# Two transformer blocks on one core: four stages' pipelines rewritten, the last stage's sum of residual and last bias on VectorE

## The chip, the cores and the metric

One of the eight cores of a Trainium2 chip runs the whole program. The metric is the device time of one execution in microseconds, lower is better. Three executions of the kernel before took 4201.59, 4202.47 and 4207.68 us; the median, 4202.47, is its time.

## The reference

Input x is 4 x 1024 x 512 in fp32 (4096 rows of 512). Block 0 is a transformer block: layer norm modulated by the condition, attention with 16 heads of 32 and a distance bias, output projection, layer norm, an MLP of 2048 with tanh gelu. Block 1 is of the same size with ternary weights and activations rounded to 8 bits by row:

```python
def act_quant(x):
    s = 127.0 / jnp.clip(jnp.max(jnp.abs(x), axis=-1, keepdims=True), EPS)
    return jnp.clip(jnp.round(x * s), -128, 127) / s
def bitlinear(x, w, b):
    return act_quant(x) @ weight_quant(w).T + b
...
# block 0, behind its attention
x = x + out @ Wout
h2 = layer_norm(x, ln2_g, ln2_b)
x = x + (gelu(h2 @ W1 + b1) @ W2 + b2)
# block 1
qkv = bitlinear(adaln(x, c, g1, w_ada1, b_ada1), w_qkv, b_qkv)
...
x = x + bitlinear(o, w_proj, b_proj)
h = gelu(bitlinear(adaln(x, c, g2, w_ada2, b_ada2), w_fc1, b_fc1))
x = x + bitlinear(h, w_fc2, b_fc2)
```

adaln is an RMS norm times g, times (1 + scale), plus shift; scale and shift are a bitlinear of the condition, one row per batch element.

## The kernel before, in words

The program is raw: each engine (TensorE "pe", VectorE "dve", ScalarE "act", GpSimd "pool", SyncE "sp" that issues all DMAs) has its own list of instructions in a fixed order, and waits on semaphores by hand. `settle` is an engine's wait for its own last counted result. Six stages follow one another with a barrier of all engines between them; results pass through scratch in HBM. Rows are handled in tiles of 128 x 512, 32 of them (NT), or in 8 blocks of 512 rows.

1. **A**, the first projection (about 0 to 320 us), and 2. **attention 0** (to 1410 us): not touched. 5. **Attention 1** (2714 to 3800 us): not touched.

3. `stage_mlp0` has two parts. **C**, `stage_outproj` (L684 to L860): for each tile, load the attention's rows o (L727) and x (L729), transpose o (L763), split it into a high and a low half (ScalarE L790, VectorE L812), twelve matmuls with the halves of Wout (L772), add x (VectorE L833), statistics (L835, L837), the root of the variance (start on VectorE L638, power on POOL L642, three more small steps on VectorE L647 to L651), normalise (L821), transpose (L779), gain and bias (four ScalarE passes, L800), high half on POOL (L854), low half on VectorE (L828), store both (L754). POOL also adds b2 to the residual (L849), and SP stores that as x1 (L745). Beside this, 18 pieces of weights (Wout, W1, W2, 512 KB each) are loaded into two raw buffers (L712) and split, high half on ScalarE (L717), low half on VectorE (L722), one piece every second step. In a step SP issues the tile's loads first, then the store of x1, then the piece's load, then the halves' stores. The split that uses the piece is in the same step. Low halves `lo` have three buffers.

**M**, `stage_fc0` (L863 to L1147): for each block of 512 rows, 16 slices f of the hidden width: twelve matmuls of fc1 (L989), gelu and high half on ScalarE (L1044, L1048), low half gl on VectorE (L1127), and two slices later twelve matmuls of fc2 into four accumulators (L1000). VectorE also works through a list of ternary weight pieces, one a slice (L1056 to L1081), whose loads SP issues one slice ahead (L926); for two of the weights TensorE has small matmuls of its own (L1020). At a block's end VectorE adds the four accumulators to x (L1133) and at once, through the one buffer xb2, x plus the projection's bias (L1140), each after the store of the one before. SP stores x2 and x2b alternately (`store_x2`, L974 to L981), ahead of the next piece's load.

4. **D**, `stage_qkv1` (L1253 to L1475): RMS norm, rounding, transposition and q, k, v for each tile. The bias enters as one more matmul in each sum: 6 rows, the products of three bf16 pieces of the bias (`bias_rows`, L1153) and three pieces of the inverse scale of the row (`inverse_pieces`, POOL, L1182). Its operands are `brow`, 6 x n, and `rT`, 6 x 128, which TensorE transposes from rc (L1295) and ScalarE copies (L1346), beside the copy of the rounded tile (L1347). The matmuls are L1303 (four) and L1304 (the bias).

6. **F**, `stage_mlp1` (L1478 to L1841): for each tile, round the attention's row (largest entry L1694, step L1699 and L1701, ScalarE L1627, VectorE L1713), transpose (L1550), project (L1559), add the residual (L1722), square (ScalarE), root on POOL (L1816 to L1824), times G, normalise (L1730, L1735), round, transpose (L1569, scales L1570), fc1 in two halves of two groups (L1581, each with a 3-row fp32 bias matmul L1582), gelu (L1657), round h (L1662, L1713), transpose in two halves (L1590), fc2 in two halves of eight matmuls (L1599), output (L1760). Three VectorE operations `scale` (L1704, L1751) multiply a step by the weight's mean; two (L1741, L1743) make the pieces of the inverse scale. POOL adds the last bias bf2 to the residual x3 into the output buffer (L1834). The bias of fc1 is split in two fp32r pieces by VectorE (L1807, L1809) in step 1, one row is placed by a DMA (L1529), and SP loads fc2's weights, three batch elements' G and shift, and tile 3 behind that. The lists run in steps s: at step s an engine handles tile s of its first job, and older tiles of later ones.

Of the kernel before, what the change touches and what calls it, by code (L numbers as in the profile page):

```python
# [636 lines left out]
def rstd_start(K, v, var, scale, eps, s_var):  # L637
    K.nc.vector.tensor_scalar(v, var, scale, eps, ALU.mult, ALU.add).then_inc(*s_var.up())  # L638


def rstd_pow(K, r, v, s_pow):
    K.nc.gpsimd.tensor_tensor(r, v, K.mhalf[:, 0:1], ALU.pow).then_inc(*s_pow.up())  # L642


def rstd_end(K, v, r, t):
    nc, dve = K.nc, K.dve
    nc.vector.tensor_scalar(t, r, r, v, ALU.mult, ALU.mult).then_inc(*dve.own.up())  # L647
    dve.settle()
    nc.vector.tensor_scalar(t, t, -0.5, 1.5, ALU.mult, ALU.add).then_inc(*dve.own.up())
    dve.settle()  # L650
    nc.vector.tensor_tensor(r, r, t, ALU.mult).then_inc(*dve.own.up())  # L651
    dve.settle()


# [30 lines left out]
def stage_outproj(K, w1h, w1l, w2h, w2l, raw_b):  # L685
    nc, a, pe, dve, act, pool, sp = K.nc, K.a, K.pe, K.dve, K.act, K.pool, K.sp
    with Stage(K, "C") as S:
# [3 lines left out]
        o_l, x_l = S.loads("oC", 3, [P, D]), S.loads("xC", 4, [P, D])  # L691
# [4 lines left out]
        st = [S.sb(f"statC{i}", [P, 12]) for i in range(4)]  # L696
        hT = [S.sb(f"hTC{i}", [P, DC, P]) for i in range(2)]
        hi, lo = S.stores("hChi", 3, [P, DC, P], F32R), S.stores("hClo", 3, [P, DC, P], F32R)
# [3 lines left out]
        s_To, s_oh, s_ol, s_mm, s_x, s_var, s_pow, s_xh, s_Tx, s_hT, s_hi, s_lo, s_xb = (S.sem() for _ in range(13))  # L702
# [21 lines left out]
        def load_tile(i):  # L724
            rows = slice(i * P, (i + 1) * P)
            o, s = o_l.take(sp, i, 1, (s_To, i + 1))
            nc.sync.dma_start(o[:], K.o_s[rows, :]).then_inc(*s.up(16))  # L727
            x, s = x_l.take(sp, i, 1, (s_xh, i + 1), (s_xb, i + 1))
            nc.sync.dma_start(x[:], a["x"].rearrange("b l d -> (b l) d")[rows, :]).then_inc(*s.up(16))  # L729

        def sync_program():
            load_w(0)
            load_tile(0)
            load_w(1)
            for dst, src in ((g2, a["L0_cond_ln2_g_cols"]), (b2, a["L0_cond_ln2_b_cols"]), (b2b, a["L0_cond_b2"].partition_broadcast(P))):
                nc.sync.dma_start(dst[:], src).then_inc(*s_vec.up(16))
            load_tile(1)
            for s in range(NT + 4):
                if s + 2 < NT:
                    load_tile(s + 2)  # L740
                if 0 <= s - 2 < NT:
                    i = s - 2
# [3 lines left out]
                if s % 2 == 0 and 2 + s // 2 < len(pieces_w):  # L746
                    load_w(2 + s // 2)
                if 0 <= s - 4 < NT:
                    i = s - 4
                    rows = slice(i * P, (i + 1) * P)  # L750
                    sp.wait_ge(s_lo, i + 1)
                    for buf_r, half in ((hi, "hi"), (lo, "lo")):
                        buf, sem = buf_r.of(i)
                        nc.sync.dma_start(K.h2_s[half][:, rows].rearrange("(c p) t -> p c t", p=P), buf[:].bitcast(F32)).then_inc(*sem.up(16))  # L754
            for r in (xb, hi, lo):
                r.done(sp)

        def tensor_program():
            for s in range(NT + 4):
                if s < NT:  # L760
                    ps, o = po_r.take(pe, s, (s_ol, s + 1)), o_l.ready(pe, s)
                    for c in range(DC):
                        op = nc.tensor.transpose(ps[:, c * P:(c + 1) * P], o[:, c * P:(c + 1) * P], K.ident[:])  # L763
                    op.then_inc(*s_To.up())
                if 0 <= s - 1 < NT:
                    i = s - 1
                    ps = pm_r.take(pe, i, (s_x, i + 1))
                    pe.wait_ge(s_ol, i + 1)
                    pe.wait_ge(s_wlo, 2)
# [1122 lines left out]
```

## Time and profile before

| | |
|---|---|
| median of three executions | 4202.47 us |
| the profiled execution | 4206.6 us, its span 4204.8 us |
| TensorE busy | 3877.2 us, 92% of the span |
| VectorE, ScalarE, POOL busy | 2793.8, 2670.9, 899.6 us |
| TensorE's mean granted clock | 0.957 of 2.4 GHz |
| DMA | 419.49 MB, mean 100 GB/s |

How to read it: PE is TensorE's matmuls, PEld its weight loads, which can run beside matmuls; DVE is VectorE, ACT ScalarE, SPq the DMA queue of SyncE. PEclk is the granted clock, 1.00 for 2.4 GHz and 0.50 for 1.2 GHz, or a mean of both over a stretch. A matmul's record is longer than the distance to the next one, because they are pipelined: the distance between starts is what one costs. "idle before" is the time an engine stood before the instruction, with the one it waited for.

### The profile page before, as it was taken

How to read it: one execution, taken by the hardware profiler on the slowest of the kernel's cores; microseconds unless marked ns; L12 is line 12 of the kernel's file. 1: busy time of each engine (PE TensorE's matmuls, PEld its weight loads, DVE VectorE, ACT ScalarE, POOL GpSimd, SP SyncE). 2: the span in 40 equal slices, each digit the busy share in tenths (PEclk: the TensorE clock that was granted, in tenths of full speed). 3: DMA queues.
4: the chain of work that ended last, by engine and by line, in shares of the span. 5: the costliest groups of instructions: out<-in, count | busy, mean ns of one | idle time of the engine just before them, and what ended most of it. 6: DMA issues, size and time to landing. Idle time of an engine off the chain costs nothing. (4 is left out here: it accounts for less than half of the span.)

```text
span 4204.8 us, 70173 instructions
## 1 busy us (share of the span) xinstructions
PE 3877.2 (92%) x26756; PEld 2571.4 (61%) x26756; DVE 2793.8 (66%) x5147; ACT 2670.9 (64%) x4699; POOL 899.6 (21%) x1188
## 2 busy tenths in 40 slices
PE   8998999999999755689999969799999999997999
PEld 7885666666666444577778854366666666663444
DVE  4327888888888565434431227688888888886887
ACT  2227888888888422222222217598888888885887
POOL 0005555555555222100000016400000000002221
PEclk9998999999999877899999989899999999997999
DMA  5445333323232355434431226732323323214221
GB/s 185 182 164 129 64 64 74 67 59 64 59 64 47 104 170 169 148 126 150 150 115 51 76 71 245 263 75 59 64 61 73 69 59 64 59 29 136 69 70 43
DMA packets 307495, 419.49 MB, mean 100 GB/s; under 512 B 89365, under 2 KB 165673, under 8 KB 307159
## 3 DMA queue, kind: packets, MB, share of 16 engines
q1 hardware_dynamic: 307162, 415.00, 35.4%
q8 instruction: 215, 3.52, 0.4%
q14 instruction: 118, 0.97, 0.1%
HBM read 257.31 MB, written 157.32 MB: 99 GB/s over the span
## 5 line engine op out<-in xcount | busy, mean ns | idle before, releaser
L555 ACT ACTIVATE Sn<-Sn,mn 128x1024 f32<-128x1024 f32 x1024 | 1174.8, 1147 | 30.4 <-DVE mn L583 18.7
L521 PEld LDWEIGHTS pt<-ident,Sn 128*128 128x128 f32 x8192 | 880.9, 141 | 420.9 <-issue 412.9
L521 PE MATMUL pt<-ident,Sn 128*128 128x128 f32 x8192 | 1123.6, 280 | 1.6 <-DVE PT L547 0.9
L545 ACT ACTIVATE PT<-pt 128x512 f32<-128x512 f32 x1280 | 737.2, 597 | 236.9 <-PE pt L521 236.8
L489 PE MATMUL sp<-KS,QS 97*128 97x512 f32 (+1 forms) x2048 | 733.8, 440 | 44.4 <-DMA KS<-s_khi 22.9
L583 DVE CUSTOM_DVE_ANT_0 Sn<-sp,biastile 128x1024 f32<-128x1024 f32 x512 | 624.5, 1220 | 145.1 <-PE sp L489 113.5
L585 DVE TENSOR_SCALAR_CACHE_REDUCE Sn<-sp 128x1024 f32<-128x1024 f32 x512 | 624.3, 1220 | 136.6 <-PE sp L489 136.4
L628 POOL TENSOR_SCALAR biastile<-dist,ascale 128x1024 f32<-128x1024 f32 x512 | 573.9, 1121 | 499.7 <-DVE mn L583 484.9
L510 PE MATMUL po<-PT,Vp 128*32 128x256 f32 x8192 | 651.5, 391 | 0.0
L547 DVE COPY PT<-pt 128x512 f32<-128x512 f32 x768 | 531.3, 692 | 118.5 <-PE pt L521 118.5
L1044 ACT ACTIVATE gf<-pf,b1T 128x512 f32<-128x512 f32 x128 | 88.1, 688 | 562.0 <-PE pf L989 535.9
L1208 POOL TENSOR_TENSOR Gada<-Gada,gada 128x512 f32<-128x512 f32 x8 | 10.1, 1268 | 1915.5 <-DMA Sada<-s_emb 1915.5
L510 PEld LDWEIGHTS po<-PT,Vp 128*32 128x32 f32 x8192 | 163.1, 108 | 343.6 <-issue 341.2
L1127 DVE TENSOR_TENSOR gl<-gf,gh 128x512 fp32r<-128x512 f32 x128 | 88.4, 693 | 381.8 <-ACT gh L1048 380.0
L489 PEld LDWEIGHTS sp<-KS,QS 97*128 97x128 f32 (+1 forms) x2048 | 312.0, 193 | 48.2 <-issue 42.3
L1000 PE MATMUL pacc<-w2h,gh 128*128 128x512 f32 x512 | 204.9, 400 | 13.4 <-DVE gl L1127 13.4
L1000 PE MATMUL pacc<-w2l,gh 128*128 128x512 f32 x512 | 204.9, 400 | 0.0
L1000 PE MATMUL pacc<-w2h,gl 128*128 128x512 f32 x512 | 204.5, 399 | 0.0
L555 ACT ACTIVATION_READ_ACCUMULATOR Sn<-Sn,mn 128x1 f32 x1024 | 201.3, 197 | 0.0
L772 PE MATMUL pCm<-wo_hi,oChi 128*128 128x512 f32 x128 | 51.6, 540 | 122.9 <-DVE oClo L812 122.9
L362 DVE SCALAR_TENSOR_TENSOR qstage<-pA,qstage 128x512 fp32r<-128x512 f32 x64 | 44.2, 690 | 165.0 <-ACT qstage L298 165.0
L989 PE MATMUL pf<-mhi,w1h 128*128 128x512 f32 x512 | 143.6, 403 | 0.0
(230 smaller groups left out, 4923.3 us busy)
## 6 DMA issues: line engine op xcount, KB each, us to landing
QS<-s_qhi SPq DMA_DIRECT2D x128, 256.0 KB, 5.1
KS<-s_khi SPq DMA_DIRECT2D x128, 256.0 KB, 7.1
KS<-s_klo SPq DMA_DIRECT2D x64, 256.0 KB, 6.1
QS<-s_qlo SPq DMA_DIRECT2D x64, 256.0 KB, 6.9
Vp<-s_v SPq DMA_DIRECT2D x64, 256.0 KB, 7.9
s_o<-og SPq DMA_DIRECT2D x32, 512.0 KB, 8.7
xA<-in_x SPq DMA_DIRECT2D x8, 1024.0 KB, 5.8
s_qhi<-qstage SPq DMA_DIRECT2D x32, 256.0 KB, 2.0
```

Of the source, the lines that this page charges most:

```text
L489: op = nc.tensor.matmul(ps[:, g * BLK:(g + 1) * BLK], qs[0:rows_s, j, t * P:(t + 1) * P], ks[0:rows_s, j, g * BLK:(g + 1) * BLK], start=Tr ...
L510: op = nc.tensor.matmul(po[g * HD:(g + 1) * HD, :], v[:, kb, j * HD:(j + 1) * HD], pT[n % 2][:, kb, g * QW:(g + 1) * QW], start=kb == 0, s ...
L521: op = nc.tensor.transpose(ps[:, i, :], sn[:, (g * HALF + i) * P:(g * HALF + i + 1) * P], K.ident[:])
L545: nc.scalar.activation(dst, src, ACT.Copy).then_inc(*s_cp_act.up())
L547: nc.vector.tensor_copy(dst, src).then_inc(*s_cp_dve.up())
L555: nc.scalar.activation(sn[:], sn[:], ACT.Exp, scale=-1.0, bias=mn[n % 3][:, t:t + 1], accum_out=sums[n % 5][:, t:t + 1]).then_inc(*s_exp.up())
L583: nc.vector.tensor_tensor_reduce(sn[:], sp_r.at[s][:], bt[s % 2][:], 1.0, 3.4e38, ALU.add, ALU.min, m).then_inc(*s_min.up())
L585: nc.vector.tensor_scalar(sn[:], sp_r.at[s][:], 1.0, None, ALU.mult, ALU.min, m).then_inc(*s_min.up())
L628: nc.gpsimd.tensor_scalar(bt[s % 2][:], dist[:, t, :], K.ascale[:, n % H:n % H + 1], 1.0, ALU.mult, ALU.mult).then_inc(*s_bias.up())
L989: op = nc.tensor.matmul(ps[:], w[:, d, f * P:(f + 1) * P], x[:, d, :], start=n + d == 0, stop=n == 2 and d == DC - 1)
L1000: op = nc.tensor.matmul(pacc[t][:], x[:, t * P:(t + 1) * P], w[:, f, :], start=f == 0 and n == 0, stop=f == FC - 1 and n == 2)
L1127: nc.vector.tensor_tensor(gl[u % 3][:], gf[u % 2][:], gh[u % 3][:], ALU.subtract).then_inc(*s_gl.up())
```

## The change

The work computed is the same. Part by part:

- **C**: SP issues a weight piece's load one split ahead and first in the step (piece 3 + s/2 at even s; the split of 2 + s/2 is unchanged). Loads of o and x are issued apart, three and two steps ahead, at the step's end; x has five buffers. The whole inverse root goes to POOL (five operations, `inverse_root`), whose other job is the sum x + b2. The high half of the normalised tile goes from POOL to ScalarE. Consumers are moved to later steps (TAIL 9 for 4). `lo` has two buffers instead of three, the statistics eight instead of four.
- **M**: the four sums x + bias are made one a step in steps 2 to 5 of the next block (`with_bias`), their stores (`store_x2b`) likewise. After the last block SP first issues the four stores of x2, then the four of x2b. The load of x moves from step 4 to step 8 of a block.
- **D**: the bias matmul has 128 rows, all but six of them zero. `brow` is 128 x 1536 and is cleared by a VectorE memset ahead of the split, rc is 128 x 128, cleared once by POOL, and is transposed and copied with the tile as a fifth block of xT; `rT` and its copy go.
- **F**: the same for fc1's bias, now in D's form: three bf16 pieces, 128 rows, `brow` 128 x 2048. The two pieces of the inverse scale (VectorE) become D's five POOL operations; the three `scale` operations go from VectorE to POOL. The sum of x3 and bf2 goes from POOL to VectorE, behind `times_g`. VectorE's list is reordered and each job works on an older tile; ScalarE's order of round_o, copy_oT and copy_hT changes; TensorE's steps are renumbered; TAIL 8 for 7.

```diff
@@ C: sync_program
-            load_tile(1)
-            for s in range(NT + 4):
-                if s + 2 < NT:
-                    load_tile(s + 2)
...
+            load_o(2)
+            load_w(2)
+            for s in range(NT + TAIL):
+                if s % 2 == 0 and 3 + s // 2 < len(pieces_w):
+                    load_w(3 + s // 2)
...
-                if s % 2 == 0 and 2 + s // 2 < len(pieces_w):
-                    load_w(2 + s // 2)
...
+                if s + 3 < NT:
+                    load_o(s + 3)
+                if s + 2 < NT:
+                    load_x(s + 2)
@@ C: vector_program, after
+            for s in range(NT + TAIL):
+                if 0 <= s - 2 < NT:
+                    i = s - 2
+                    dve.wait_ge(s_x, i + 1)
+                    nc.vector.bn_stats(st[i % 8][:, 0:6], x_l.at[i][0][:]).then_inc(*s_bn.up())
+                if s < NT:
+                    o_low(s)
...
+                if s % 2 == 0 and 2 + s // 2 < len(pieces_w):
+                    split_lo(2 + s // 2)
+                if 0 <= s - 6 < NT:
+                    h_low(s - 6)
+                if 0 <= s - 1 < NT:
+                    residual(s - 1)
+                if 0 <= s - 3 < NT:
+                    normalise(s - 3)
@@ M: store_x2, store_x2b, with_bias
+                nc.sync.dma_start(K.x2_s[rows_of(i, t), :], x_l.at[i, t][0][:]).then_inc(*s_xst.up(16))
+
+        def store_x2b(i, t):
+            sp.wait_ge(s_xb, TPB * i + t + 1)
+            nc.sync.dma_start(K.x2b_s[rows_of(i, t), :], xb2[:]).then_inc(*s_xbst.up(16))
...
+                if u >= FC + 2 and 0 <= u % FC - 2 < TPB:
+                    with_bias(u // FC - 1, u % FC - 2)
@@ bias_rows
-    rows, rest = S.sb("brow" + name, [6, n], BF16), S.sb("brest" + name, [6, n])
+    rows, rest = S.sb("brow" + name, [P, n], BF16), S.sb("brest" + name, [6, n])
...
+        nc.vector.memset(rows[:], 0.0).then_inc(*dve.own.up())
@@ D: project
-            nc.tensor.matmul(pr[w][:], rT[i % 2][:], brow[:, cols], start=False, stop=True).then_inc(*s_m[w].up())
+            nc.tensor.matmul(pr[w][:], xT[i % 2][:, DC, :], brow[:, cols], start=False, stop=True).then_inc(*s_m[w].up())
@@ F: times_g and gpsimd_program
             nc.vector.tensor_tensor(xn[i % 3][:], x3[i % 4][:], G[:, b, :], ALU.mult).then_inc(*s_xg.up())
+            dve.wait_ge(s_bf2, 16)
+            buf = xo.room(dve, i)
+            nc.vector.tensor_tensor(buf[:], x3[i % 4][:], bf2[:], ALU.add).then_inc(*s_xb.up())
...
-                nc.gpsimd.tensor_tensor(buf[:], x3[i % 4][:], bf2[:], ALU.add).then_inc(*s_xb.up())
```

In F, VectorE's list after the change is, in step s: largest_o(s), quantise h(s-6), quantise x(s-4), largest_h(s-5, 0), times_g(s-3) with the new sum, largest_h(s-5, 1), step_o(s), step_h(s-5), normalise(s-3), output(s-7), largest x(s-3), quantise o(s-1), step x(s-3), residual(s-2), and in step 1 the bias split at the end. TensorE's is: turn_h(s-4, 0), turn_x(s-2), fc2(s-5, 1), turn_o(s), fc1(s-2, 0), turn_h(s-4, 1), project(s), fc1(s-2, 1), fc2(s-4, 0).

## Rows read from the trace of the kernel before

**Rows 1.** Windows of stages C, M, D, F: length, busy (instructions), PEclk, DMA share, GB/s.

```profile
1405.00:1715.00 310.00, 161.76 (x690) 127.95 (x679) 175.94 (x340) 81.50 (x179) 76.29 (x96) 0.74 0.56 169
1715.00:2490.00 775.00, 731.64 (x3108) 588.11 (x3108) 241.79 (x356) 170.19 (x257) 0.00 (x0) 0.97 0.31 105
2490.00:2710.00 220.00, 172.19 (x896) 76.66 (x896) 149.99 (x296) 136.00 (x288) 126.39 (x356) 0.89 0.68 249
...
3795.00:4204.80 409.80, 378.72 (x2138) 175.26 (x2130) 324.99 (x742) 296.95 (x386) 93.39 (x196) 0.95 0.27 82
```

**Rows 2.** Waits in stage C, 1440 to 1680 us: total, times, longest.

```profile
ACT w1h L717 <- DMA wraw<-in_L_cond_W: 94.3, 7, 14.1
```

**Rows 3.** Timeline of stage C: start, us, what, idle before.

```profile
1541.22 0.42 SPq L712 DMA_DIRECT2D wraw<-in_L_cond_W  x1
...
1545.79 1.06 ACT L717 ACTIVATE w2h<-wraw 128x1024 fp32r<-128x1024 f32 x1 [13.20 <-DMA wraw<-in_L_cond_W]
```

**Rows 4.** Groups by line, stage C, 1440 to 1680 us: busy, mean ns, idle before.

```profile
L833 DVE TENSOR_TENSOR xC<-pCm,xC 128x512 f32<-128x512 f32 x27 | 18.4, 682 | 0.0
...
L722 DVE TENSOR_TENSOR w2l<-wraw,w2h 128x1024 fp32r<-128x1024 f32 x7 | 8.6, 1226 | 47.0 <-ACT w2h L717 47.0
```

**Rows 5.** The transpositions of o in stage C: ns min/median/max, first and last start.

```profile
L763 PE MATMUL pCo<-ident,oC x128: 272/273/475, 1416.8 to 1685.1; 128*128 128x128 f32 x128
```

**Rows 6.** Waits of TensorE in stage M, 1715 to 2490 us.

```profile
PE pacc L1000 <- DVE gl L1127: 13.4, 3, 5.2
PE pmisc L1020 <- DVE tern L1081: 11.8, 1, 11.8
```

**Rows 7.** Timeline at the end of stage M.

```profile
2488.34 0.32 SPq L981 DMA_DIRECT2D s_x2b<-xb  x1
...
2490.47 0.69 DVE L1140 TENSOR_TENSOR xb<-xM,bpb 128x512 f32<-128x512 f32 x1 [2.15 <-DMA s_x2b<-xb]
```

**Rows 8.** Timeline of one tile's step in stage D.

```profile
2620.21 0.40 PE L1294 MATMUL pxD<-identb,xqD 128*128 128x128 bf16 x4
...
2622.57 0.09 PEld L1304 LDWEIGHTS pqD<-browD,rTD 6*128 6x128 bf16 x1 [0.42 <-issue]
...
2622.89 1.04 PE L1303 MATMUL pkD<-wtqkv,xTD 128*128 128x512 bf16 x4
...
2625.47 0.40 PE L1294 MATMUL pxD<-identb,xqD 128*128 128x128 bf16 x4
```

**Rows 9.** The chain that ended last, one tile of stage F: start, share in us.

```profile
4054.29 1.83 PE p2F L1599 x8
...
4056.90 1.73 PE p2F L1599 x8
...
4064.23 0.97 PE pwF L1581 x4
4065.20 0.42 PE pwF L1582
4065.62 1.83 PE p2F L1599 x8
```

**Rows 10.** Groups by line of VectorE, stage F, 4000 to 4100 us.

```profile
L1730 DVE TENSOR_TENSOR xnF<-x3F,Gada 128x512 f32<-128x512 f32 x9 | 6.1, 682 | 0.0
...
L1704 DVE TENSOR_SCALAR smF<-smF,wmean 128x1 f32<-128x1 f32 x27 | 5.4, 200 | 0.0
```

**Rows 11.** Windows in stage F's head and steady part, columns as rows 1.

```profile
3820.00:3880.00 60.00, 49.72 (x223) 20.56 (x223) 45.20 (x110) 38.38 (x54) 15.77 (x34) 0.77 0.40 129
...
4020.00:4090.00 70.00, 70.00 (x400) 32.96 (x400) 61.73 (x144) 56.98 (x76) 18.06 (x40) 1.00 0.27 76
```

**Rows 12.** Timeline of stage F's head.

```profile
3817.15 2.28 DVE L1809 TENSOR_TENSOR blowF<-brawF,browF 3x2048 fp32r<-3x2048 f32 x1
...
3833.90 0.69 DVE L1694 TENSOR_REDUCE smF<-oF 128x1 f32<-128x512 f32 x1 [7.45 <-DMA oF<-s_o]
...
3839.72 0.40 PE L1569 MATMUL pxF<-identb,xqF 128*128 128x128 bf16 x4 [0.58 <-DVE xqF L1713]
```

More of the change, by code:

```diff
@@ new lines, in turn_o, with project @@
+        def turn_o(i):
+            ps, o = po_r.take(pe, i, (s_ol, i + 1)), o_l.ready(pe, i)
+            for c in range(DC):
+                op = nc.tensor.transpose(ps[:, c * P:(c + 1) * P], o[:, c * P:(c + 1) * P], K.ident[:])
+            op.then_inc(*s_To.up())
+        def project(i):
+            ps = pm_r.take(pe, i, (s_x, i + 1))
+            pe.wait_ge(s_ol, i + 1)
+            pe.wait_ge(s_wlo, 2)
+            for n, (x, w) in enumerate(((oh[i % 2], wo_hi), (oh[i % 2], wo_lo), (ol[i % 2], wo_hi))):
+                for d in range(DC):
+                    op = nc.tensor.matmul(ps[:], x[:, d, :], w[:, d, :], start=n + d == 0, stop=n == 2 and d == DC - 1)
+            op.then_inc(*s_mm.up())
@@ new lines, in turn_h @@
+        def turn_h(i):
+            ps = px_r.take(pe, i, (s_hT, i + 1))
+            pe.wait_ge(s_xh, i + 1)
+            for c in range(DC):
+                op = nc.tensor.transpose(ps[:, c * P:(c + 1) * P], xh[i % 2][:, c * P:(c + 1) * P], K.ident[:])
+            op.then_inc(*s_Tx.up())
+        def tensor_program():
+            for s in range(NT + TAIL):
+                if 0 <= s - 2 < NT:
+                    project(s - 2)
+                if 0 <= s - 5 < NT:
+                    turn_h(s - 5)
+                if s < NT:
+                    turn_o(s)
@@ new lines, in o_high, with affine @@
+        def o_high(i):
+            act.wait_ge(s_To, i + 1)
+            if i >= 2:
+                act.wait_ge(s_mm, i - 1)
+            nc.scalar.activation(oh[i % 2][:], po_r.at[i][:].rearrange("p (c t) -> p c t", t=P), ACT.Copy).then_inc(*s_oh.up())
+        def affine(i):
+            act.wait_ge(s_vec, 48)
+            if i >= 2:
+                act.wait_ge(s_lo, i - 1)
+            act.wait_ge(s_Tx, i + 1)
+            for c in range(DC):
+                op = nc.scalar.activation(hT[i % 2][:, c, :], px_r.at[i][:, c * P:(c + 1) * P], ACT.Identity,
+                                          bias=b2[:, c:c + 1], scale=g2[:, c:c + 1])
+            op.then_inc(*s_hT.up())
@@ L782, in scalar_program, with h_high @@
+        def h_high(i):
+            buf = hi.room(act, i)
+            act.wait_ge(s_hT, i + 1)
+            nc.scalar.activation(buf[:], hT[i % 2][:], ACT.Copy).then_inc(*s_hi.up())
         def scalar_program():
@@ L856, in stage_outproj @@
+        def gpsimd_program():
+            pool.wait_ge(s_vec, 48)
+            for i in range(NT):
+                inverse_root(i)
+                buf = xb.room(pool, i)
+                nc.gpsimd.tensor_tensor(buf[:], x_l.at[i][0][:], b2b[:], ALU.add).then_inc(*s_xb.up())
         sync_program()
@@ L955, in sync_program @@
                     store_x2(i - 1)
+                if i > 0 and 0 <= f - 2 < TPB:
+                    store_x2b(i - 1, f - 2)
                 if u + 1 < len(work):
@@ L1452, in gpsimd_program @@
         def gpsimd_program():
+            for buf in rc:
+                nc.gpsimd.memset(buf[:], 0.0).then_inc(*pool.own.up())
+            pool.settle()
             pool.wait_ge(s_winv, 1)
@@ L1621, in tensor_program @@
                     fc2(s - 5, 1)
+                if s < NT:
+                    turn_o(s)
+                if 0 <= s - 2 < NT:
+                    fc1(s - 2, 0)
+                if 0 <= s - 4 < NT:
+                    turn_h(s - 4, 1)
+                if s < NT:
+                    project(s)
+                if 0 <= s - 2 < NT:
+                    fc1(s - 2, 1)
+                if 0 <= s - 4 < NT:
+                    fc2(s - 4, 0)
         def round_o(i):
```

382 lines of the change are left out of this document (164 added, 218 removed).

## The prediction

> **What bounds the kernel now.** Read the windows first, one for each stage that the change edits, because a share over the whole span would mix six stages [rows 1]. Together the four take 1714.8 of 4204.8 us; the rest, the first projection and the two attentions, isn't touched and is taken at no change. The profiled execution took 4206.6 us (span and 1.8 us around it); that is 4.1 above the median of 4202.5, so I work against 4206.6 and take 4.1 off at the end.
>
> The four rows differ in kind. Stage C (output projection) keeps nobody busy: TensorE 162 of 310 us at a granted clock of 0.74, VectorE 176, DMA share 0.56. M, D and F keep TensorE busy for 94%, 78% and 92%. So C must be read for a wait, D and F for TensorE's cost per tile.
>
> C's waits: ScalarE stands 94.3 us before seven splits of W1's pieces, waiting for the piece's load, and W2's pieces alternate with them [rows 2]. The timeline shows why: the load is issued at 1541.22 and ScalarE starts 4.6 us later, having stood 13.2 us [rows 3]. SP issues it behind the tile loads and a store that wait on results of the last step, and the split that needs it stands ahead of the step's other work. First to last transposition takes 1685.1 - 1416.8 = 268.3 us, 8.65 a tile [rows 5].
>
> **Part 1, stage C.** The load is now issued one split (two steps) ahead, at the head of a step; VectorE's chain for the inverse root goes to POOL, with later consumers. The 13 us wait goes. What is late next? Per tile:
> - DMA: 0.56 x 310 = 174 us, 5.4 a tile at a share of 1. Same bytes afterwards.
> - TensorE: 161.8 x 0.74 = 120 us at full clock, 3.7 a tile; about 7.5 if granted only 1.2 GHz.
> - VectorE: five passes near 0.7 (two low halves, the residual, the statistics, the normalisation), half a split of 1.23, aggregation 0.2: 4.3 [rows 4].
> - ScalarE 81.5/32 = 2.5, plus a high half that it takes from POOL, 0.6: 3.1. POOL 76.3/32 = 2.4, less that pass, plus four small operations: near 3.
>
> DMA is highest. I take 6.0 us a tile (DMA share 0.9); ends 5.4 and 7.0. Gain 31 x 2.65 = 82. After the last transposition the stage now runs on for 30 us with split waits in it; I estimate 22. **C: -90** (-108 to -55). The ring of low halves is cut from three to two; its store has about two steps to land, so I cost it at nothing, and at steps under 5.4 it would bind first.
>
> **Part 2, stage M.** At each block's end VectorE makes four biased sums through one buffer, each behind the last one's store. TensorE loses 11.8 + 13.4 us behind that at four block ends [rows 6]. The sums move to the next block's steps, one a step. SP, however, still stores the four residual tiles one after another ahead of the next weight load, so only the sums' share goes: the third sum and store repeat after 2.13 + 0.69 + 0.03 = 2.85 us [rows 7], stores alone after about 2.1 + 0.35. With the last pair's store gone too, some 4 us a block end return: -15 for four. At the stage's end it turns round. Now all four residual stores (3 x 2.45 more) come before the first of the biased ones, still 2.85 apart: the last is issued about 5 us later than now, with no work to hide it. **M: -10** (-17 to +2). The later load of the residual tile (step 8) has seven steps for a load of a few us: nothing.
>
> **Part 3, stage D.** The bias matmul has 6 rows, afterwards 128 (zeros below). Its weight load comes after 0.42 us of idle, instead of during the matmul before, and from it to the next group pass 2622.89 - 2622.57 = 0.32 us [rows 8], where a matmul of this width takes 1.73/8 = 0.216 [rows 9]. The group before it ends 0.1 late too, as 0.97 for 0.86 in rows 9. So 0.2 is lost, three times a tile. D's step, 2625.47 - 2620.21 = 5.26, falls by 0.6 to 4.66. Cover: VectorE 150/32 = 4.7 busy (its head split included), POOL 3.9, ScalarE 4.2 less one small copy, DMA 0.68 x 220/32 = 4.7 [rows 1]. All are near, so I take 4.75: 31 x 0.5 = 15.5. The new memset of 128x1536 before the bias split lies on the head's path: no row shows it; nearest are passes of 0.7 to 1.2, lower bound 0, upper 2, taken 1.5. The 128-column transposition of the scales costs nothing visible. **D: -14** (-20 to -3).
>
> **Part 4, stage F.** TensorE's order of work is the same sequence, only its steps are renumbered. Its cost per tile is the distance of two equal rows of the chain, 11.33 us [rows 9], with TensorE busy 70 of 70 us at clock 1.00 [rows 11]. The 3-row fp32 bias matmul takes 0.42 for 0.216, and what follows it pays 0.10: four matmuls 0.97 for 0.86, eight 1.83 for 1.73 [rows 9]. That is 0.30 four times a tile: -1.20, and 0.05 for the fp32 transposition of the scales. TensorE then needs 10.08: 32 x 1.25 = **-40**.
>
> Does VectorE follow? It is busy 61.7 of 70 us, 9.99 a tile [rows 11]. It loses two pieces of the inverse scale and three scales, about 0.2 each (-1.0), and gains the sum of residual and last bias, 0.68 as the product of the same shape [rows 10]: 9.7. So it still lies under 10.08, by 0.4. On POOL, 93 of 410 us busy [rows 1], that sum has room; on VectorE it costs 0.68 of the scarcest cover, but nothing on the path while TensorE bounds. I add 0.1 a tile for this nearness: **+3**.
>
> The head loses. The bias for fc1 is now split in three pieces: memset, two casts, two subtractions over 2048 columns instead of one each. A subtraction takes 2.28 [rows 12], a cast about half: 7.0 against 3.5. A memset comes on top, which no row shows: 0.3 to 2.28 as that subtraction, taken 1.3. It starts some 1.5 earlier, ahead of the second residual. So it ends 3 later. SP waits for it, then places three rows (not one), and only then loads fc2's weights, the modulation rows and tile 3. VectorE already stands 7.45 us for tile 3, until 3833.90 [rows 12]; I get 3838.5. In the kernel before, tile 1's transposition is then ready at 3839.7. In the longer pipeline tile 0 is only normalised behind tile 3's reduction, some ten passes, 7 us. Its fc1 and a projection follow, 24 matmuls at 1.2 GHz, 0.43 each: 10 us. Only then comes tile 1, at 3855.8, 16 us later with nothing to hide it: **+16** (5 to 22). **F: -21** (-36 to +2).
>
> **Sum.** -90 - 10 - 14 - 21 = -135: 4206.6 - 135 = 4071.6, less 4.1: 4067 us.
>
> **A rule against parts 3 and 4.** The rows show the short weight load standing idle. The Trainium skill, "TensorE: Matmul & The Clock Gate", "LDWEIGHTS (loading the stationary operand)", says that a load costs by its columns, not its rows; by that alone 128 rows for 6 gain nothing. The same page, in the steps of a matmul, lets a load run ahead when row groups don't conflict or it goes to the background buffer, which leaves the gap unexplained. By the rule alone the sum would be rival 1's.
>
> **Rivals.**
> 1. *The padded matmul keeps its gap.* For it: both shapes have 128 columns. Against: loads of full height run ahead in the same stream, and a group's four matmuls keep 0.216. Then D and F lose 15 + 40 of their gains: 4067 + 55 = 4122. Chance 0.03.
> 2. *VectorE bounds F.* POOL's thirteen operations are those that D has, 3.9 us a tile. If 1.6 of that delays VectorE, a tile takes 11.3 and F gains nothing but its head: +37, 4104. Against: D's VectorE keeps up under the same load. 0.12.
> 3. *C at the low clock.* If the gaps keep TensorE often at 1.2 GHz, or SP's waits hold back transfers, a tile takes 7.0: +31, 4098. For it: clock 0.74 now. 0.14.
> 4. *Better.* C at 5.4 and a head that hides: -18 - 16, 4033. 0.10.
> 5. *Slower.* Stage F falls to the low clock and stays: at a mean grant c a tile takes 10.08/c. F's head had 0.77 while TensorE was busy 50 of 60 us [rows 11]. At 0.5 it is 20.2 a tile, +284 + 16 against 114 gained elsewhere: about 4390. It decides from 10.08/c = 14.4, c = 0.70. Against: TensorE stays over 95% busy in the steady part. 0.01.
>
> Forecast: 0.60. A measurement of this kernel can tell about 0.2% (8 us) from no change. The four terms' ends add up to 4021 and 4148, were all to fall one way, which isn't likely; the range 4028 to 4108 leaves out rival 1, rival 5 and a little of each tail. Faster 0.98, same 0.01, slower 0.01.
>
> **What would show it.** C: transpositions 6.0 apart, no ScalarE wait for weight loads of over 1 us, DMA share near 0.9. M: the 11.8 wait down to 8, last biased store 5 later after the last matmul. D: 4.7 a tile, no idle before L1304's successor. F: 10.1 to 10.2 a tile, TensorE full, VectorE waiting under 0.5 a tile, second tile's transposition about 53 us after the stage's first load (now 37). I am wrong if C's step stays over 7, or if F's is over 10.6.

## The result, and the profile of the kernel after

The kernel after takes 4012.8 us (median of four runs, 4008.7 to 4015.2) against 4202.7 for the kernel before (4201.6 to 4207.7): a ratio of 0.9545, with a 95% interval of 0.9528 to 0.9561. It is 190 us faster. The forecast was 135 us faster, 4067 with a range of 4028 to 4108; the result lies 15 us below the range. The profiled execution took 4015.2 us, its span is 4013.4.

Counted from one stage's first transfer to the next one's, in the two profiled executions (us):

| stage | before | after | difference | forecast |
|---|---|---|---|---|
| C | 303.3 | 171.5 | -131.8 | -90 |
| M | 783.5 | 764.3 | -19.2 | -10 |
| D | 214.9 | 200.8 | -14.1 | -14 |
| F | 401.9 | 373.8 | -28.1 | -21 |
| all others | 2501.2 | 2503.0 | +1.8 | 0 |

Nine tenths of the miss lie in C and M, and three quarters of it in C alone. How far a stage moves from kernel to kernel without any edit to it is told by the kernels below that are the kernel after except in another stage: C 168 to 174, M 762 to 769, F 372 to 376.

The windows of the four stages in the kernel after, to be read beside [rows 1], with the same columns:

```profile
1407.00:1587.00 180.00, 135.29 (x682) 101.60 (x674) 128.91 (x212) 102.14 (x211) 116.62 (x192) 0.91 0.91 291
1587.00:2342.00 755.00, 725.01 (x3108) 583.07 (x3108) 241.51 (x357) 170.60 (x257) 0.00 (x0) 0.98 0.32 108
2342.00:2552.00 210.00, 151.40 (x896) 83.65 (x896) 148.46 (x296) 136.37 (x257) 128.29 (x358) 0.87 0.75 264
3632.00:4013.40 381.40, 331.06 (x2130) 172.66 (x2122) 317.84 (x616) 293.78 (x354) 172.21 (x422) 0.93 0.27 88
```

C changed its kind: the DMA share went from 0.56 to 0.91, the clock from 0.74 to 0.91. And here is the first sign of what was wrong: share times length is 164 us, where the forecast had taken 174 as a quantity that no edit could lower, and the rate rose from 169 to 291 GB/s, more than the share did.

C's transpositions (durations, first and last start; [rows 5] before) and its longest waits, 1440 to 1555 us:

```profile
L751 PE MATMUL pCo<-ident,oC x128: 270/273/476, 1418.5 to 1559.1; 128*128 128x128 f32 x128
```

```profile
ACT oChi L783 <- PE pCo L751: 20.4, 25, 2.1
...
DVE hClo L823 <- DMA s_h2lo<-hClo: 20.0, 13, 2.6
ACT hTC L791 <- DVE hClo L823: 18.4, 19, 1.7
POOL xbC L879 <- DMA s_x<-xbC: 13.0, 14, 1.7
```

A tile takes 140.6 / 31 = 4.53 us, not 6.0. The wait of ScalarE for weight pieces is gone [rows 2]. What ends waits now is a store: VectorE stands for a buffer of low halves until its store has landed (20.0 us), and ScalarE stands behind VectorE for nearly as long. POOL stands 13.0 us for a buffer of its sum x + b2, until that store has landed, and for nothing else but its own last results.

The end of M [rows 7]:

```profile
2332.95 0.40 PE L1033 MATMUL pacc<-w2h,gl 128*128 128x512 f32 x1
2334.06 0.68 DVE L1144 TENSOR_TENSOR xb<-xM,bpb 128x512 f32<-128x512 f32 x1
2338.68 9.19 SPq L1014 DMA_DIRECT2D s_x2b<-xb  x4
2341.12 0.69 DVE L1144 TENSOR_TENSOR xb<-xM,bpb 128x512 f32<-128x512 f32 x1 [6.38 <-DMA s_x2b<-xb]
...
2349.95 0.32 SPq L1285 DMA_DIRECT2D xD<-s_x  x1
```

The second biased sum waits 6.38 us, because the first one's store is issued behind four residual stores. From the last matmul to the next stage's first transfer pass 17.0 us (12.8 before).

F's chain, the starts of the same group of eight matmuls in two tiles ([rows 9] before), and its head ([rows 12]):

```profile
3867.49 0.86 PE pwF L1612 x4
3868.36 0.22 PE pwF L1613
3868.57 1.73 PE p2F L1630 x8
...
3878.60 1.73 PE p2F L1630 x8
```

```profile
3639.57 0.34 SPq L1544 DMA_DIRECT2D oF<-s_o  x1
...
3652.03 0.91 DVE L1201 MEMSET browF<- 128x1024 uint32 x1 [0.16 <-issue]
...
3675.58 0.69 DVE L1725 TENSOR_REDUCE smF<-oF 128x1 f32<-128x512 f32 x1 [13.55 <-DMA oF<-s_o]
...
3681.76 0.61 PE L1600 MATMUL pxF<-identb,xqF 128*128 128x128 bf16 x4 [15.85 <-DVE xqF L1741]
...
3691.57 0.39 PE L1600 MATMUL pxF<-identb,xqF 128*128 128x128 bf16 x4
```

A tile takes 10.03 us for 11.33, every group of four matmuls 0.86 and every bias matmul 0.22. The second tile's transposition comes 52.0 us after the stage's first transfer (36.8 before).

### The profile page after: what moved, and what is told of

Same layout as the page of the kernel before. It is cut to its first block and busy times, and to the rows that moved or that the text cites. A ratio compares the mean times of both kernels' runs of the same rounds, so it can differ in the third digit from the quotient of the medians.

```text
span 4013.4 us, 70190 instructions
## 1 busy us (share of the span) xinstructions
PE 3777.5 (94%) x26756; PEld 2544.7 (63%) x26756; DVE 2737.7 (68%) x4895; ACT 2689.1 (67%) x4667; POOL 1023.3 (25%) x1512
## 5 line engine op out<-in xcount | busy, mean ns | idle before, releaser
L1077 ACT ACTIVATE gf<-pf,b1T 128x512 f32<-128x512 f32 x128 | 88.3, 690 | 536.2 <-PE pf L1022 526.9
```

## The experiments

Each kernel was compared with the kernel before on the same chip. The stages are parted by barriers, so a kernel is read by its own stage's length: the total alone would blur it by the 2 to 6 us that the other stages move. In the code, `...` marks what is left out.

**1. Is C's gain the wait for the weight pieces?** One kernel is the old one with the load moved alone, the other the new one with the load put back.

```diff
@@ wait_alone, from the kernel before
+            load_w(2)
             for s in range(NT + 4):
+                if s % 2 == 0 and 3 + s // 2 < len(pieces_w):
+                    load_w(3 + s // 2)
...
-                if s % 2 == 0 and 2 + s // 2 < len(pieces_w):
-                    load_w(2 + s // 2)
@@ wait_back, from the kernel after
-            load_w(2)
             for s in range(NT + TAIL):
-                if s % 2 == 0 and 3 + s // 2 < len(pieces_w):
-                    load_w(3 + s // 2)
...
+                if s % 2 == 0 and 2 + s // 2 < len(pieces_w):
+                    load_w(2 + s // 2)
```

> The kernel before with one edit: a weight piece's load is issued one split earlier and first in its step; order of work, root of the variance and rings as before. Theory 1 (the wait for pieces is nearly all of C's loss, so DMA transfers then carry the step): C falls from 303 us to 190 or less, the whole by 100 to 130 us. Theory 2 (the wait hides a second loop of nearly its length, the chain statistics, root, normalise, transpose, split across four engines, which the longer pipeline cuts): C only falls to 230 to 260, the whole by 40 to 70 us.

> The kernel after with one edit undone: the piece's load is issued in the step of its split again, behind the store of x1. Theory 1: the split waits some 8 us every second step again, C goes from 171 us to 270 or more, the whole 100 to 130 us slower than the kernel after (ratio to before 0.98 or more). Theory 2: the longer pipeline has most of the gain, C stays at 200 to 230 (ratio 0.962 to 0.970).

wait_alone: 4105.7 us, ratio 0.9764 (0.9749 to 0.9778), C 201.6 us. wait_back: 4075.5 us, 0.9694 (0.9679 to 0.9708), C 233.9. Neither theory in its pure form: from 303 us the load alone gives 102 and the rest of the edit alone 69, and both together 132. wait_alone by itself is already 12 us below what the forecast had for the whole of C (201.6 for 213). Its transpositions come 169.1 / 31 = 5.45 us apart. Here is its window 1450 to 1540, and under it four of VectorE's groups there (busy, mean ns, idle before):

```profile
1450.00:1540.00 90.00, 67.16 (x318) 52.58 (x317) 85.52 (x169) 40.25 (x88) 37.84 (x49) 0.94 0.89 279
```

```profile
L651 DVE TENSOR_TENSOR statC<-statC 128x1 f32<-128x1 f32 x16 | 11.8, 735 | 0.6
...
L647 DVE TENSOR_SCALAR statC<-statC 128x1 f32<-128x1 f32 x16 | 4.4, 273 | 1.1
...
L649 DVE TENSOR_SCALAR statC<-statC 128x1 f32<-128x1 f32 x16 | 2.5, 154 | 0.6
L638 DVE TENSOR_SCALAR statC<-statC 128x1 f32<-128x1 f32 x16 | 2.5, 154 | 0.6
```

VectorE is busy 85.5 of 90 us. The four small operations of the inverse root, which the change gives to POOL, take 21.2 / 16 = 1.3 us a tile, more than half of it in a product of one column (735 ns; the last section shows that this is mostly a wait for POOL). With the wait for pieces gone, VectorE is the next bound. Taking 1.3 us a tile from it is what these rows name as the way below 5.45; no kernel moves the chain alone, so how the other 30 us (201.6 to 171.5) part between the chain, the later consumers and the deeper buffers isn't shown.

**2. What sets 4.53 us?** Three theories: the rate of all transfers, the two buffers of low halves, VectorE. One kernel stores less, one more, one has three buffers again, and one has both.

```diff
@@ less_bytes (VectorE's wait for the buffer goes too; M loads the high halves twice)
-                    for buf_r, half in ((hi, "hi"), (lo, "lo")):
+                    for buf_r, half in ((hi, "hi"),):
...
@@ more_bytes (a buffer of xb is free when both stores have landed)
-        xb = S.stores("xbC", 2, [P, D])
+        xb = S.stores("xbC", 2, [P, D], n_dma=2)
...
                     nc.sync.dma_start(K.x1_s[i * P:(i + 1) * P, :], buf[:]).then_inc(*sem.up(16))
+                    nc.sync.dma_start(K.x2_s[i * P:(i + 1) * P, :], buf[:]).then_inc(*sem.up(16))
@@ lo3; lo3_more is lo3 with the edit of more_bytes
-        st = [S.sb(f"statC{i}", [P, 12]) for i in range(8)]
+        st = [S.sb(f"statC{i}", [P, 12]) for i in range(4)]
-        hi, lo = S.stores("hChi", 3, [P, DC, P], F32R), S.stores("hClo", 2, [P, DC, P], F32R)
+        hi, lo = S.stores("hChi", 3, [P, DC, P], F32R), S.stores("hClo", 3, [P, DC, P], F32R)
...
```

> The kernel after without the store of h2's low halves in C (M reads the high halves twice, so it moves the same bytes; the low term of h2 is left out of the output). C moves 44.0 MB for 52.4. Theory DMA (bytes at full rate set the step): transpositions 3.8 us apart for 4.53, C 22 to 25 us shorter. Theory ring (the two low buffers' wait sets the step): also shorter, as the wait goes with the store. Theory VectorE (its passes set the step): under 5 us.

> The kernel after with the sum x + b2 stored twice in C (the second time to the place of x2, which is written again later): 60.8 MB for 52.4. Theory DMA: 5.25 us a tile, C 22 to 25 us longer. Theory ring: some 0 to 10 us longer, by later landings alone. Theory VectorE: under 3 us.

> The kernel after with three buffers for the low halves in C again (the statistics get four instead of eight, which nothing waits for). Theory ring (the landing of a store into one of two buffers sets the step of 4.53 us): the step falls to VectorE's 4.1, C 10 to 13 us shorter. Theory rate (all transfers together are at their limit, the ring only shows it): step 4.4 to 4.5, C 0 to 4 us shorter.

> Three buffers for the low halves as in lo3, and x + b2 stored twice as in more_bytes: 60.8 MB in C. Theory rate (the transfers of the core are at a limit near 380 GB/s, which lo3 at 4.23 us a tile and 1.64 MB has just reached): 1.90 MB a tile take 5.0 us, C 22 to 25 us longer than in lo3. Theory ring (only buffers that wait for landings, here the two of x + b2, set the step, and VectorE else): 4.3 to 4.6 us a tile, C 2 to 12 longer than in lo3.

The fifth column is the mean from the first to the last transposition. The sixth is the mean of 20 tiles in the middle, between the ends of POOL's 9th and 29th sum x + b2, where nearly every tile has all its transfers; the last is what POOL stands in it, a tile, for a store of that sum to land.

| kernel | total, us | ratio (95%) | C, us | us a tile | middle tiles | POOL's wait for the store |
|---|---|---|---|---|---|---|
| after | 4012.8 | 0.9545 (0.9528 to 0.9561) | 171.5 | 4.53 | 4.69 | 0.50 |
| less_bytes | 4001.2 | 0.9519 (0.9505 to 0.9534) | 156.7 | 4.11 | 4.21 | 0.01 |
| more_bytes | 4029.0 | 0.9579 (0.9563 to 0.9595) | 187.3 | 5.01 | 5.27 | 1.12 |
| lo3 | 4002.7 | 0.9526 (0.9511 to 0.9540) | 163.2 | 4.23 | 4.34 | 0.14 |
| lo3_more | 4022.9 | 0.9571 (0.9557 to 0.9586) | 178.7 | 4.73 | 5.00 | 0.91 |

The step follows the bytes, but by 15 us where the rate theory asked for 22 to 25; and the third buffer alone gives 8 (10 in the whole, where the two intervals overlap; in C, 163.2 lies clear of the 168 to 174 of kernels without an edit there). Both the ring and the transfers have a part. The windows 1450 to 1540 of after, lo3 and less_bytes:

```profile
1450.00:1540.00 90.00, 77.63 (x387) 58.13 (x385) 72.43 (x124) 59.53 (x124) 71.51 (x117) 1.00 1.00 326
```

```profile
1450.00:1540.00 90.00, 82.52 (x418) 63.61 (x418) 84.05 (x136) 64.72 (x136) 76.54 (x124) 1.00 1.07 359
```

```profile
1450.00:1540.00 90.00, 84.46 (x432) 66.36 (x430) 88.30 (x138) 67.53 (x143) 79.59 (x128) 1.00 0.98 310
```

In less_bytes transfers no longer fill the time (310 GB/s). VectorE is busy 88.3 of 90 us there. But none of the three theories names POOL, which since the change has a list of six operations a tile in C. The group of its sum in the same window, in after, less_bytes and the kernel of the next experiment (busy, mean ns, idle before):

```profile
L879 POOL TENSOR_TENSOR xbC<-xC,b2b 128x512 f32<-128x512 f32 x19 | 25.5, 1342 | 9.9 <-DMA s_x<-xbC 9.8
```

```profile
L879 POOL TENSOR_TENSOR xbC<-xC,b2b 128x512 f32<-128x512 f32 x22 | 28.8, 1308 | 1.0 <-DMA s_x<-xbC 0.8
```

```profile
L883 POOL TENSOR_TENSOR xbC<-xC,b2b 128x512 f32<-128x512 f32 x21 | 27.1, 1292 | 0.0
```

POOL's other idle time is 0.08 to 0.11 us before each small operation, its `settle`. It never stands for an input in the middle tiles: with the settles its list fills everything but the wait for a store, 4.20 us a tile in after (4.69 - 0.50), in less_bytes and in lo3. So less_bytes, at 4.21, runs at the pace of that list, and its 15 us are what lies between after and that pace. How much of the 4.20 is POOL's own isn't known, because VectorE and POOL also hold each other up (last section). In lo3 the transfers have 359 GB/s for 326, and VectorE is busy 84 us; its other 6.0 are a wait for POOL's inverse root:

```profile
L835 DVE TENSOR_SCALAR xhC<-xC,statC 128x512 f32<-128x512 f32 x21 | 22.7, 1081 | 6.0 <-POOL statC L872 6.0
```

Does VectorE hold lo3? The next kernel takes work from it.

**3. Is it VectorE in lo3?** The normalisation goes to ScalarE.

```diff
@@ norm_act, from lo3 (POOL makes w = -mean * r)
-            nc.vector.tensor_scalar(xh[i % 2][:], x_l.at[i][0][:], t[:, 6:7], t[:, 9:10], ALU.subtract, ALU.mult).then_inc(*s_xh.up())
+            nc.scalar.activation(xh[i % 2][:], x_l.at[i][0][:], ACT.Identity, bias=t[:, 10:11], scale=t[:, 9:10]).then_inc(*s_xh.up())
...
```

> lo3 with the normalisation of C moved from VectorE to ScalarE (one activation with scale and bias, POOL makes the bias in one more small operation). VectorE loses 1.08 us a tile of 3.95 busy. Theory VectorE bounds lo3: step falls from 4.23 to 3.9 or less, C 10 us or more shorter. Theory rate: step stays at 4.1 to 4.25, C within 4 us of lo3. ScalarE then has 3.3 to 3.7 us a tile.

4007.6 us, 0.9538 (0.9523 to 0.9554), C 164.4, the tile (1546.6 - 1415.2) / 31 = 4.24 us. VectorE fell to 76.2 of the 90 us, and nothing came of it. Its window:

```profile
1450.00:1540.00 90.00, 81.71 (x420) 64.92 (x419) 76.23 (x115) 76.11 (x158) 78.53 (x146) 1.00 1.06 360
```

The rate is 360 GB/s again. So less work on VectorE alone doesn't shorten the step. It doesn't clear VectorE wholly, because the edit also gives POOL a seventh operation, and POOL is now full: its sum has 0.0 idle before it, and its list takes 4.33 us a tile in the middle, the whole step (lo3: 4.34, of which the list 4.20 and the store 0.14). What is shown is that two things stand at the step of lo3 at once, POOL's list and, by the next experiment, the rate.

**4. The disputed term by itself.** Three stages of nothing but C's transfers run ahead of C, each transfer waiting for the last one of its own buffer only.

```diff
@@ moves, from the kernel after
+        stage_moves(K, w1h, raw_b, "Z", dict(o=3, x=5, b=2, h=3, l=2))
+        stage_moves(K, w1h, raw_b, "Y", dict(o=3, x=5, b=2, h=3, l=3))
+        stage_moves(K, w1h, raw_b, "X", dict(o=6, x=6, b=6, h=6, l=6))
         stage_outproj(K, w1h, w1l, w2h, w2l, raw_b)
```

> The kernel after with three extra stages ahead of C that only move C's bytes (per tile: o and x loaded, x1 and both halves stored, half a weight piece: 1.57 MB, in C's shapes, zeros stored), each transfer waiting only for the last one of its own buffer: first with C's rings (two low-half buffers), then with three of them, then with six of everything but the weights. They measure the disputed term itself. The prediction's floor: 5.4 us a tile in all three. Theory ring: the first takes 4.3 to 4.5 us a tile, the second 3.9 to 4.2, the third 3.5 to 4.0, and C's 4.53 and lo3's 4.23 stand just above the first and second. Theory rate: all three within 0.2 of each other, at 4.1 to 4.3, and C's 4.53 comes from the way the transfers are spread in time. If all three are under 3.9, transfers by themselves set neither, and the loop of waits through the engines does.

The issues of x1's stores in the three stages, and the windows between the first and the last of them (one execution, 4471.7 us in all, the three stages in it):

```profile
L705 SPq DMA_DIRECT2D s_x<-bZ x32: 429/549/1538, 1416.2 to 1552.3; - x32
...
L705 SPq DMA_DIRECT2D s_x<-bY x32: 432/524/1443, 1566.4 to 1704.0; - x32
...
L705 SPq DMA_DIRECT2D s_x<-bX x32: 441/606/1359, 1723.5 to 1859.7; - x32
```

```profile
1416.20:1552.30 136.10, 0.00 (x0) 0.00 (x0) 0.00 (x0) 0.00 (x0) 0.00 (x0) 0.50 1.06 353
1566.40:1704.00 137.60, 0.00 (x0) 0.00 (x0) 0.00 (x0) 0.00 (x0) 0.00 (x0) 0.50 1.06 351
1723.50:1859.70 136.20, 0.00 (x0) 0.00 (x0) 0.00 (x0) 0.00 (x0) 0.00 (x0) 0.50 1.07 352
```

136.1 / 31 = 4.39 us a tile, 4.44 and 4.39: the same with two, three or six buffers, at 351 to 353 GB/s. That is a rate, not a ring, and it stands at a share of 1.06, not at 1. Beside work the core moved a little more: 359 in lo3, 360 in norm_act, 366 in lo3_more, in the same window. Now the middle tiles can be read. In lo3 a tile takes 4.34 us, about what the bare transfers take, and just above POOL's 4.20. After, with two low buffers, takes 4.69 at 326 GB/s. A second store makes 1.84 MB a tile, for which the bare rate asks 5.1 us (worked out: 4.39 x 1.84 / 1.57); more_bytes takes 5.27 and lo3_more 5.00. The means between first and last transposition lie lower, because that stretch has fewer bytes a tile: the stores lag four to seven tiles behind, and the last weight piece is issued in step 28. Why work beside the transfers goes with a slightly higher rate stays open.

The Trainium skill, "DMA: Bandwidth & Descriptors", "Where 436 GB/s comes from", gives about 358 GB/s as one core's share of HBM and says that this binds transfers between HBM and SBUF, with a larger value for a core alone; the 351 to 366 GB/s of the runs here lie near the 358, though only one core is at work.

**5. M: are the block ends the biased sums?** They go back to the block's end, stored by turns.

```diff
@@ m_back, from the kernel after
-                    store_x2(i - 1)
-                if i > 0 and 0 <= f - 2 < TPB:
-                    store_x2b(i - 1, f - 2)
+                    store_pairs(i - 1)
...
+                    for t in range(TPB):
+                        with_bias(i, t)
-                if u >= FC + 2 and 0 <= u % FC - 2 < TPB:
-                    with_bias(u // FC - 1, u % FC - 2)
```

> The kernel after with M's four biased sums at the block's end again and stored by turns with the residual tiles (the later load of the residual stays). Theory of the prediction, sized by the stage: the other seven block ends cost 23 us again, the last one 4 less: M 19 us longer than after, the whole 4032. Rival: the later load of the residual tile has part of the 23: M only 8 to 15 longer.

4029.8 us, 0.9588 (0.9574 to 0.9602), 17 more than after, and M 782.4 us, 18 more. The later load of the residual has no part that can be seen. TensorE's waits in M, first of after, then of m_back ([rows 6] has 13.4 and 11.8):

```profile
PE pmisc L1053 <- DVE tern L1114: 7.8, 1, 7.8
PE pacc L1033 <- DVE gl L1168: 1.0, 2, 0.6
```

```profile
PE pacc L1037 <- DVE gl L1172: 14.3, 3, 5.2
PE pmisc L1057 <- DVE tern L1118: 11.5, 1, 11.5
```

The three waits of 13.4 us in all shrink to 1.0 in after and come back whole.

**6. D and F: is it the height of the bias matmul?** Both operands are cut to the six rows that aren't zero, and nothing else.

```diff
@@ short_rows, from the kernel after; the same in D
-                op = nc.tensor.matmul(pw[n][:, g * D:(g + 1) * D], xT[i % 2][:, DC, :], brow[:, cols], start=False, stop=True)
+                op = nc.tensor.matmul(pw[n][:, g * D:(g + 1) * D], xT[i % 2][0:6, DC, :], brow[0:6, cols], start=False, stop=True)
```

> The kernel after with the bias matmuls of D and F reading only the six rows that are not zero (both operands cut to six rows, the zeros stay where they are). Theory gap (a short weight load isn't drawn ahead, 0.2 us lost for each): D's tile 0.5 longer, 15 us in all, as before the change; F's four a tile make 10.03 into 10.8, 25 us; the whole 35 to 42 us slower than after. Theory that the row count does nothing: under 2 us, and the gain of D and F came from their other edits.

4052.2 us, 0.9639 (0.9623 to 0.9655), 39 more than after. The two stages have 36 of it: F 398.2 for 373.8, D 211.9 for 200.8. A stretch of F's timeline in short_rows, then in after:

```profile
3861.74 0.09 PEld L1613 LDWEIGHTS pwF<-browF,xTF 6*128 6x128 bf16 x1 [0.42 <-issue]
3861.74 0.39 PE L1613 MATMUL pwF<-browF,xTF 6*128 6x512 bf16 x1
3862.06 1.04 PE L1612 MATMUL pwF<-wtfc,xTF 128*128 128x512 bf16 x4
```

```profile
3863.43 0.10 PEld L1613 LDWEIGHTS pwF<-browF,xTF 128*128 128x128 bf16 x1
3863.65 0.38 PE L1613 MATMUL pwF<-browF,xTF 128*128 128x512 bf16 x1
3863.86 1.03 PE L1612 MATMUL pwF<-wtfc,xTF 128*128 128x512 bf16 x4
```

The short load starts with its own matmul, behind 0.42 us of standing; the full one 0.22 ahead of it, beside the matmul before. By the starts, 0.32 us pass to the next group for 0.21, and the group ahead is 0.1 longer too (0.97 for 0.86 in F's chain). Both loads last the same, 0.09 and 0.10 us: the rule of the Trainium skill, "TensorE: Matmul & The Clock Gate", "LDWEIGHTS (loading the stationary operand)", that a load costs by its columns, agrees with these records. It doesn't tell when the load starts, and that is the only difference that these rows show.

**7. The sum on VectorE or on POOL.** The part of the change that its name mentions is undone alone.

```diff
@@ pool_sum, from the kernel after: out of times_g, into gpsimd_program behind inverse_root
-            nc.vector.tensor_tensor(buf[:], x3[i % 4][:], bf2[:], ALU.add).then_inc(*s_xb.up())
+                    nc.gpsimd.tensor_tensor(buf[:], x3[(s - 3) % 4][:], bf2[:], ALU.add).then_inc(*s_xb.up())
```

> The kernel after with the sum of residual and last bias in F on POOL again, behind the inverse root. Theory TensorE bounds F: VectorE falls from 67 to about 62 of 70 us busy and the stage's steady tile stays 10.03; the whole within 3 us. Theory nearness (VectorE at 96% holds TensorE up in places): 3 to 6 us faster. Theory POOL late (its small operations for the steps come later behind the sum, and it slows VectorE at the port): 5 to 30 us slower.

4015.0 us, 0.9554 (0.9539 to 0.9568), F 372.8 us: no difference. 70 us of F's steady part in after and in pool_sum:

```profile
3850.00:3920.00 70.00, 70.00 (x456) 37.11 (x454) 67.06 (x133) 62.93 (x76) 36.95 (x91) 1.00 0.25 77
```

```profile
3853.00:3923.00 70.00, 70.00 (x456) 37.11 (x454) 62.58 (x127) 62.95 (x78) 38.59 (x100) 1.00 0.27 80
```

VectorE goes from 67.1 to 62.6 us and TensorE stays at 70 of 70. VectorE at 96% costs nothing here (the totals, 4015.0 and 4012.8, are within each other's intervals).

**8. Three repairs together.**

```diff
@@ v_all, from the kernel after: lo3's edit in C, and
@@ M: the last block's stores, x2 and x2b of each tile by turns
-            store_x2(NBLK - 1)
-            for t in range(TPB):
-                store_x2b(NBLK - 1, t)
+            store_pairs(NBLK - 1)
@@ F: sync_program
+            load_tile(3)
             place_bias()
+            load_tile(4)
...
-            for s in range(NT + TAIL):
+            for s in range(2, NT + TAIL):
```

> The kernel after with three repairs, one for each stage: lo3 in C; after M's last block the stores of residual and biased sum by turns as before the change; in F tile 3 is loaded ahead of the placing of the bias rows and tile 4 ahead of fc2's weights. By stages: C 8 to 10 shorter, M 4 to 5 shorter (from the last matmul to the next stage 12.8 us for 17.0). F: theory that tile 3's landing holds the head: VectorE's 13.6 us of waiting for it go and F falls from 374 to 360 to 365; theory that the bias split, the weights and the longer pipeline hold it: F within 3 us. The whole 3987 to 4000.

3989.0 us (3986.1 to 3991.1), ratio 0.9491 (0.9477 to 0.9506): the fastest, 24 us under after, their intervals apart. C 162.4, M 760.5, F 362.5. From M's last matmul to the next stage it is 12.8 us again (2333.44 - 2320.66). F's head, where the stage's first transfer is at 3624.63:

```profile
3653.56 0.61 PE L1608 MATMUL pxF<-identb,xqF 128*128 128x128 bf16 x4 [3.70 <-DVE xqF L1749]
```

The first tile's transposition comes 28.9 us after it (42.2 in after), and F gets 11.3 of those 13.3 us: the late load of tile 3, with tile 4 behind it, did hold the head.

## Why the prediction was wrong, step by step

**C, forecast -90, measured -132: the step that failed.** It is the line "DMA: 0.56 x 310 = 174 us, 5.4 a tile at a share of 1", and the fill of 0.9 laid on top, which made 6.0. The share isn't work that stays the same. Before, 169 GB/s went at a share of 0.56, and 169 / 0.56 = 302; the bare transfers move 353 at 1.06, or 333 for a share of 1, and they pass 1. So the floor of the transfers for a tile of 1.57 MB is 4.4 us, not 5.4, and the mean tile in C is lighter still. And the share wasn't 0.9 but 0.97 between first and last transposition, at 315 GB/s. Of the 127.7 us between those, 82 were forecast; the run after the last transposition fell by 4 (30.7 to 26.5), forecast 8.

Of the other statements on C, three held. The wait for the pieces was there and went; but alone it would have brought 5.45 us a tile, with VectorE full. The forecast's order of bounds put VectorE's 4.3 under DMA's 5.4; in after it is busy 72.4 of 90 us. "At steps under 5.4 it would bind first", said of the low halves' ring, is what happened: it costs some 8 us in C, costed at nothing because the step was thought to be 6.0. Rival 3, the low clock, fell with the step: the granted clock is 1.00 in C's steady part. One did not hold, "POOL ... near 3": its list takes 4.20 us a tile, 3.75 of them busy. Under a step of 6.0 that would have cost nothing; at 4.69 it is the nearest bound behind the transfers, and less_bytes runs at its pace.

**M, forecast -10, measured -19.** The mechanism was right, its size off. The term "only the sums' share goes", some 4 us a block end, supposed that four residual stores ahead of the next weight load would keep the rest of the wait. They don't: the 13.4 us fall to 1.0, and the 11.8 to 7.8. Against the end's +4.2 (forecast +5), the other block ends gave 23 us, of which these two rows show 16; the rest is within what M moves by itself. m_back returned 17 to 18 us.

**D, forecast -14, measured -14.** Its tile went from 5.63 to 5.17 us (160.4 / 31), by 0.46 for the 0.5 forecast, though from a higher place: 5.26 was read from one step. short_rows returned 11.1 us by height alone. The memset was taken at 1.5 us and takes 0.70, and the head is as long as before, 21.3 us.

**F, forecast -21, measured -28.** TensorE's tile fell by 1.30 us, 40 in all, as forecast. The head lost 15.2 of the 16. The +3 for VectorE's nearness wasn't there, as pool_sum shows; the remaining 3 us or so are within what the stage moves by itself and weren't taken apart. Rival 2 fell with the tile of 10.03 us, in which TensorE stands for nothing; rival 1 with short_rows.

Rival 4, better at 4033 with 0.10, was on the right side but not for its reasons: it had C at 5.4, the same false floor, and a head that hides, where F's head lost 15.2 us in full. C's best end was that one quotient and its likeliest value stood on it. Even with all four terms at their best ends the forecast's sum was 4021, so no part of it could reach 4013.

## What to carry to other kernels

A DMA share multiplied by a stretch's length is no amount of work. For a floor take bytes over a rate, the rate from the stretch of the same kernel where transfers stand thickest, and keep the far end of the range below it, since the share can pass 1.

When one long wait goes, rank what comes next by time a tile and ask which part of the change moves each: here the load ahead alone was worth 102 us, down to VectorE's bound; the rest of the edit, with the root's chain given to POOL, gave the next 30; one more buffer gives 8; and then the transfers (4.4 us a tile) and POOL's list (4.2) stand close together. When work is moved to an idle engine, add up that engine's whole list, with its waits for its own results, before you call it free. The bias matmuls on six rows were worth padding to full height where TensorE was the bound (36 to 39 us); the place of one cheap sum, on VectorE or on POOL, made no difference there.

## What the runs showed of the hardware that was not expected

- One core's transfers reached a limit at 351 to 353 GB/s when they were alone, whatever the number of buffers, and up to 366 beside work. In those three stages the issue of a transfer itself takes up to 1.5 us, for 0.43 at the least.
- A bias matmul on six rows starts together with its weight load, behind 0.42 us in which the load side stands; the one on 128 rows has its load 0.22 us ahead, beside the matmul before. The two loads last as long (0.09 and 0.10 us). Seven such matmuls a tile cost 36 us by the lengths of the two stages, 39 by the totals.
- VectorE and POOL take turns for some pairs of operations. The first sign was that VectorE's product of two single columns (L651) takes 735 ns in wait_alone, and that the normalisation (L835) has a mean of 577 ns in after and 1081 in lo3. Two of its starts in lo3, one of them inside POOL's sum, and two operations in less_bytes, where it is POOL that started second:

```profile
1499.71 0.53 DVE L835 TENSOR_SCALAR xhC<-xC,statC 128x512 f32<-128x512 f32 x1
...
1504.61 1.28 POOL L879 TENSOR_TENSOR xbC<-xC,b2b 128x512 f32<-128x512 f32 x1
1504.69 1.49 DVE L835 TENSOR_SCALAR xhC<-xC,statC 128x512 f32<-128x512 f32 x1 [0.85 <-POOL statC L872]
```

```profile
1494.56 1.19 DVE L705 TENSOR_TENSOR w2l<-wraw,w2h 128x1024 fp32r<-128x1024 f32 x1
1494.57 1.22 POOL L870 TENSOR_SCALAR statC<-statC 128x1 f32<-128x1 f32 x1
```

A normalisation that starts ahead of POOL's sum, or beside one of POOL's small operations, takes 0.53 us. One that starts inside the sum ends 0.28 us after the sum's end, whenever it started: so it was in all 22 cases of 1440 to 1555 in after and lo3 (3 of 25 and 19 of 27). The product L651 of wait_alone started inside POOL's sum in all 21 cases of 1440 to 1560, and ended 0.02 us after it. The other way round, a POOL operation on one column, 0.19 us elsewhere, took 1.22 because VectorE's split had started 0.01 before it, and ended 0.05 after it. Not every pair does this: VectorE's passes that read PSUM (L817, L828) and its statistics (L844) take the same 0.67 to 0.69 us beside POOL's sum as without it. In the kernels here what takes turns with POOL's sum is a VectorE pass with both operands in SBUF, or this normalisation. It makes the busy time of both engines partly a wait for the other, and it is why neither can be read alone as the bound of less_bytes.
